# DLRM tower on one core: tables from the second on are split, loaded and awaited in one part instead of two, with the four orders laid out anew

## The reference, cut to what matters

```python
# 512 samples; 26 tables of 1000 to 125000 rows x 128, fp32
e = stack([tbl_f[ids[:, f]] for f in range(26)], axis=1)        # 512 x 26 x 128
combined = concatenate([dense[:, None, :], e], axis=1)          # 512 x 27 x 128
gram = einsum('bnd,bmd->bnm', combined, combined)               # 27 x 27 dot products per sample
z = concatenate([dense, gram[:, triu_i, triu_j], dense], axis=1)  # 128 + 351 + 128 = 607
h = maximum(z @ W_top1 + b_top1, 0)                             # 512 x 512
h = maximum(h @ W_top2 + b_top2, 0)                             # 512 x 256
y = h @ W_top3                                                  # 512 x 1
```

## Time and profile before

| what | value |
|---|---|
| median of 3 runs | 109.44 us (109.06 to 109.8) |
| profiled execution | 109.33 us |
| its span in the trace | 107.4 us |
| TensorE's granted clock | 1.0 of full speed throughout |

### The profile page before, as it was taken

How to read it: one execution, slowest core, us unless ns; L and a number is a source line. 1 busy time by engine, 2 the same in 40 slices (tenths; PEclk the granted TensorE clock), 3 DMA queues, 4 the chain that set the end, 5 groups by cost and what they waited for, 6 DMA issues and landing times.

```text
span 107.4 us, 3972 instructions
## 1 busy us (share of the span) xinstructions
PE 98.3 (92%) x1657; PEld 80.4 (75%) x1657; DVE 86.0 (80%) x255; ACT 64.4 (60%) x110; POOL 64.5 (60%) x68
## 2 busy tenths in 40 slices
PE   5969897997999899998999999999999997999991
PEld 2337576764766788877899887999798866998890
DVE  4799999999999999999999999999572436078121
ACT  5699989999999997809989474846300040001210
POOL 3577778777777778777777777777777700000000
PEclk9999999999999999999999999999999999999999
DMA  2999985747567847999782852112222110000000
GB/s 59 319 288 329 396 266 169 206 135 228 168 173 236 247 146 219 329 326 315 252 279 63 227 167 55 49 49 55 55 58 67 52 31 6 0 6 0 0 6 1
DMA packets 10575, 16.19 MB, mean 151 GB/s; under 512 B 2352, under 2 KB 6478, under 8 KB 10558
## 3 DMA queue, kind: packets, MB, share of 16 engines
q1 hardware_dynamic: 8398, 11.62, 34.0%
q0 software_dynamic: 2016, 4.13, 13.3%
q10 hardware_dynamic: 144, 0.19, 0.5%
HBM read 15.94 MB, written 0.00 MB: 148 GB/s over the span
## 4 chain that ended last, share of the span: by engine, by line
POOL 57%; issue 18%; PE 15%; DMA 6%; POOLq 1%; DVE 1%; DVEq 0%
POOL rows_sb L530 57%; PE h_ps L675 3%; DMA rows_sb<-in_tbl,ids_sb 3%; PE h_ps L650 3%; DMA ids_sb<-in_ids 2%; PE gram_ps L594 2%; PE h_ps L619 1%; PE turn_ps L650 1%; POOLq L293 1%; PE gram_ps L650 1%; PE turn_ps L619 1%; PE h_ps L658 1%; PE gram_ps L611 1%; PE turn_ps L594 1%; PE place_ps L611 0%
## 5 line engine op out<-in xcount | busy, mean ns | idle before, releaser
L530 POOL DMA_INDIRECT rows_sb<-in_tbl,ids_sb x63 | 63.6, 1009 | 20.9 <-issue 18.9
L571 PE MATMUL turn_ps<-onehot_sb,high_sb 128*128 128x512 f32 (+2 forms) x118 | 41.9, 367 | 3.5 <-DVE low_sb L807 1.4
L798 DVE TENSOR_SCALAR_CACHE_REDUCE onehot_sb<-lookup_ids_sb,first_sb 128x256 fp32r<-128x256 int16 (+2 forms) x79 | 43.6, 598 | 0.0
L572 PE MATMUL turn_ps<-onehot_sb,low_sb 128*128 128x512 f32 (+2 forms) x118 | 38.9, 342 | 0.0
L571 PEld LDWEIGHTS turn_ps<-onehot_sb,high_sb 128*128 128x128 f32 x118 | 22.2, 188 | 9.5 <-DVE low_sb L807 2.4
L572 PEld LDWEIGHTS turn_ps<-onehot_sb,low_sb 128*128 128x128 f32 x118 | 22.3, 189 | 1.6
L739 ACT ACTIVATE onehot_sb<-lookup_ids_sb,first_sb 128x512 fp32r<-128x512 int16 (+2 forms) x31 | 18.8, 621 | 2.3 <-PE turn_ps L572 2.2
L807 DVE TENSOR_TENSOR low_sb<-table_sb,high_sb 128x640 fp32r<-128x640 f32 (+1 forms) x26 | 19.4, 757 | 0.0
L729 ACT CAST high_sb<-table_sb 128x640 fp32r<-128x640 f32 (+1 forms) x26 | 17.0, 672 | 3.0 <-PE turn_ps L572 2.8
L594 PE MATMUL gram_ps<-feats 128*32 128x27 f32 x960 | 12.8, 196 | 1.1 <-DVE feats L701 0.4
L747 ACT ACTIVATE onehot_sb<-onehot_sb 128x768 fp32r<-128x768 f32 (+4 forms) x13 | 13.6, 1049 | 0.1
(11 more groups left out here) (53 smaller groups left out, 74.2 us busy)
## 6 DMA issues: line engine op xcount, KB each, us to landing
table_sb<-in_tbl SPq DMA_DIRECT2D x13, 256.0 KB, 3.5
table_sb<-in_tbl SPq DMA_DIRECT2D x7, 320.0 KB, 3.6
lookup_ids_sb<-in_lookup_ids SPq DMA_DIRECT2D x12, 128.0 KB, 2.4
table_sb<-in_tbl SPq DMA_DIRECT2D x6, 192.0 KB
rows_sb<-in_tbl,ids_sb POOLq DMA_INDIRECT x63, 3.3
w1p_sb<-in_w_pairs SPq DMA_DIRECT2D x1, 768.0 KB
w1d_sb<-in_w_dense SPq DMA_DIRECT2D x1, 512.0 KB, 6.3
w_sb<-in_w SPq DMA_DIRECT2D x1, 512.0 KB, 6.0
```

Source lines behind the costliest of these rows:

```text
L530: pool.indirect_dma_start(out=rows_sb[:, GATHERS.index((tile, slot)), :], out_offset=None, in_=tables[f], in_offset=bass.IndirectOffsetOnAxis(
L571: nc.tensor.matmul(bank, high_sb[0:rows, u % 2, c, :], picked, start=c == 0, stop=False)
L572: nc.tensor.matmul(bank, low_sb[0:rows, u % 2, c, :], picked, start=False, stop=c == CHUNKS[u] - 1).then_inc(chunk_used, 1)
L798: nc.vector.tensor_scalar(onehots(u, [c])[:, 0, :], lookup_ids_at(u), row_ids_sb[:, row:row + 1], None, ALU.is_equal, ALU.add, accum_out=m ...
```

## The change

`table_parts` gives one part for every table but the first. With it, for tables 1 to 12, the rows before the last chunk come with one DMA instead of two, both DMAs of a table count on one semaphore (one wait for 32), and there is one `cast`, one `low` and one wait of TensorE ahead of chunk 0. Table 0 keeps its two halves. The chunks that VectorE and ScalarE compare are the same in number. All four orders are written anew: among much else `turn 0 0` comes ahead of lookup 1, `turn 3 0` ahead of `lookup 12 8:10`, twins and `copy turn` steps elsewhere, `merge 3 0 16` ahead of `relu1 2`, `place 2` on VectorE ahead of `copy turn 3 4` and `layer3 1`, and on SP the loads of `dn`, `w1p`, `w1d`, `sm`, `w2` and `mask` between other tables. GpSimd's program is the same.

```diff
--- before.py
+++ after.py
@@ -113,18 +113,17 @@
 ONEHOT_MAX = max(n * (B - first * P) for n, first in zip(CHUNKS, LOOKUP_FROM))
 WARM_UPS = 12
 ACT_ROWS = 2 * NPAD
-ACT_CHUNKS = [2,3]*6+[3]
+ACT_CHUNKS = [2, 3] * 6 + [3]
 
 
 def table_parts(u):
 
-    return [range(0, CHUNKS[u] // 2), range(CHUNKS[u] // 2, CHUNKS[u])]
+    return [range(0, CHUNKS[u] // 2), range(CHUNKS[u] // 2, CHUNKS[u])] if u == 0 else [range(0, CHUNKS[u])]
 
 
 def dve_chunks(u):
 
-    first, second = table_parts(u)
-    return [first, range(second.start, CHUNKS[u] - ACT_CHUNKS[u])]
+    return [range(part.start, min(part.stop, CHUNKS[u] - ACT_CHUNKS[u])) for part in table_parts(u)]
 
 
 def act_chunks(u):
@@ -221,52 +220,49 @@
 
 
 PE_ORDER = """
-    lookup 0 0:8; lookup 1 0:8; turn 0 0; lookup 2 0:7; turn 0 1; lookup 2 7; lookup 3 0:3; turn 0 2; lookup 3
-    3:8; turn 0 3; lookup 4 0:8; turn 0 4; lookup 5 0:2; turn 1 0; lookup 5 2:8; lookup 6 0:4; gram 0 0 0;
-    lookup 6 4; gram 0 0 1; lookup 6 5:10; lookup 7 0; gram 0 1 0; lookup 7 1; turn 1 1; lookup 7 2:6; turn 1 2;
-    gram 0 1 1; lookup 7 6:10; lookup 8 0:4; place 0 0 32; lookup 8 4:6; turn 1 3; lookup 8 6:10; layer1 0 0 4;
-    turn 1 4; lookup 9 0:10; turn 2 0; lookup 10 0:2; gram 1 0 0; lookup 10 2; layer2 0 0; lookup 10 3:5; gram 1
-    0 1; lookup 10 5:10; gram 1 1 0; lookup 11 0:2; turn 2 1; lookup 11 2; gram 1 1 1; lookup 11 3:10; lookup 12
-    0:2; layer2 0 1; turn 2 2; turn 2 3; lookup 12 2:10; place 1 0 32; gram 2 0 0; gram 2 0 1; layer1 1 0 4;
-    gram 2 1 0; gram 2 1 1; layer2 1 0; turn 3 0; turn 3 1; turn 3 2; place 2 0 32; layer2 1 1; turn 3 3; turn 3
-    4; gram 3 0 0; gram 3 0 1; layer1 2 0 4; gram 3 1 0; gram 3 1 1; layer2 2 0; layer2 2 1; dense1 3 0 1;
-    dense1 3 1 2; place 3 0 16; place 3 16 32; bias2 3; dense1 3 2 3; dense1 3 3 4; layer1 3 0 1; layer1 3 1 2;
-    layer1 3 2 3; layer1 3 3 4; layer2 3 0; layer2 3 1
+    lookup 0 0:8; turn 0 0; lookup 1 0:8; lookup 2 0; turn 0 1; lookup 2 1:8; lookup 3 0:8; turn 0 2; lookup 4
+    0:4; turn 0 3; lookup 4 4:8; lookup 5 0:8; turn 0 4; lookup 6 0; gram 0 0 0; lookup 6 1:7; gram 0 0 1;
+    lookup 6 7:10; turn 1 0; lookup 7 0:4; gram 0 1 0; turn 1 1; lookup 7 4:6; gram 0 1 1; lookup 7 6:10; lookup
+    8 0:4; turn 1 2; lookup 8 4; turn 1 3; lookup 8 5; place 0 0 32; lookup 8 6:10; layer1 0 0 4; turn 1 4;
+    lookup 9 0:10; lookup 10 0:5; layer2 0 0; turn 2 0; gram 1 0 0; lookup 10 5; turn 2 1; lookup 10 6:8; gram 1
+    0 1; lookup 10 8:10; lookup 11 0; gram 1 1 0; lookup 11 1; layer2 0 1; lookup 11 2:4; turn 2 2; lookup 11
+    4:10; gram 1 1 1; lookup 12 0:4; turn 2 3; lookup 12 4:8; turn 3 0; lookup 12 8:10; place 1 0 32; gram 2 0
+    0; gram 2 0 1; layer1 1 0 4; gram 2 1 0; layer2 1 0; gram 2 1 1; turn 3 1; turn 3 2; layer2 1 1; place 2 0
+    32; turn 3 3; turn 3 4; gram 3 0 0; gram 3 0 1; layer1 2 0 4; gram 3 1 0; gram 3 1 1; dense1 3 0 1; layer2 2
+    0; layer2 2 1; place 3 0 16; dense1 3 1 2; place 3 16 32; dense1 3 2 3; bias2 3; dense1 3 3 4; layer1 3 0 1;
+    layer1 3 1 2; layer1 3 2 3; layer1 3 3 4; layer2 3 0; layer2 3 1
 """
 
 ACT_ORDER = """
-    distance 0 6; cast 0 0; distance 0 7; cast 0 1; distance 1 5; cast 1 0; distance 1 6; onehot 0; distance 1
-    7; onehot 1; cast 1 1; cast 2 0; distance 2 6; copy lookup 0; cast 2 1; distance 2 7; dense; cast 3 0;
-    onehot 2; cast 3 1; distance 3 5:7; copy turn 0 0; copy lookup 1; distance 3 7; copy turn 0 1; copy lookup
-    2; cast 4 0; onehot 3; distance 4 6:8; cast 4 1; cast 5 0; copy lookup 3; distance 5 5; cast 5 1; copy turn
-    0 3; distance 5 6; onehot 4; copy turn 0 2; distance 5 7; cast 6 0; copy lookup 4; distance 6 8; onehot 5;
-    copy turn 0 4; twin 0; distance 6 9; cast 6 1; cast 7 0; copy lookup 5; twin 1; distance 7 7; onehot 6; cast
-    7 1; distance 7 8:10; distance 8 8; cast 8 0; cast 8 1; onehot 7; copy lookup 6; copy lookup 7; distance 8
-    9; onehot 8; distance 9 7; cast 9 0; distance 9 8; copy turn 1 1; distance 9 9; place 0 0 32; onehot 9; copy
-    lookup 8; distance 10 8; copy turn 1 3; distance 10 9; onehot 10; cast 9 1; cast 10 0; cast 10 1; twin 2;
-    distance 11 7:9; cast 11 0; distance 11 9; cast 11 1; onehot 11; cast 12 0; copy lookup 9; cast 12 1; copy
-    lookup 10; distance 12 7; copy turn 2 1; distance 12 8; copy lookup 11; distance 12 9; onehot 12; twin 3;
-    copy turn 2 3; copy lookup 12; place 1 0 32; place 2 0 32; copy turn 3 1; copy turn 3 3; place 3 0 16; place
-    3 16 32; relu1 3 0 1; relu1 3 2 3
+    distance 0 6:8; cast 0 0; cast 0 1; onehot 0; distance 1 5:7; cast 1 0; distance 1 7; onehot 1; distance 2
+    6:8; cast 2 0; copy lookup 0; onehot 2; copy turn 0 0; distance 3 5:7; copy turn 0 1; cast 3 0; copy lookup
+    1; distance 3 7; dense; copy lookup 2; onehot 3; distance 4 6; cast 4 0; distance 4 7; onehot 4; cast 5 0;
+    copy lookup 3; copy turn 0 2; distance 5 5:8; onehot 5; copy lookup 4; distance 6 8; copy turn 0 3; cast 6
+    0; twin 0; distance 6 9; copy lookup 5; copy turn 0 4; cast 7 0; distance 7 7; onehot 6; distance 7 8:10;
+    cast 8 0; copy lookup 6; distance 8 8:10; copy turn 1 1; onehot 7; twin 1; twin 2; copy lookup 7; onehot 8;
+    cast 9 0; distance 9 7:9; place 0 0 32; twin 3; distance 9 9; copy lookup 8; distance 10 8; onehot 9;
+    distance 10 9; onehot 10; copy turn 1 3; cast 10 0; cast 11 0; copy lookup 9; distance 11 7:10; copy lookup
+    10; distance 12 7; copy turn 2 1; distance 12 8; cast 12 0; distance 12 9; onehot 11; copy lookup 11; onehot
+    12; copy turn 2 3; copy lookup 12; place 1 0 32; copy turn 3 1; copy turn 3 3; place 2 0 32; place 3 0 16;
+    place 3 16 32; relu1 3 0 1; relu1 3 2 3
 """
 
 DVE_ORDER = """
-    onehot 0 0:4; low 0 0; low 0 1; onehot 0 4; low 1 0; onehot 0 5; onehot 1 0:5; low 1 1; onehot 2 0:4; low 2
-    0; low 2 1; onehot 2 4:6; low 3 0; low 3 1; onehot 3 0:5; onehot 4 0; low 4 0; onehot 4 1:3; low 4 1; onehot
-    4 3:6; onehot 5 0:2; low 5 0; onehot 5 2:5; low 5 1; onehot 6 0:3; low 6 0; onehot 6 3:6; copy turn 1 0; low
-    6 1; onehot 6 6:8; onehot 7 0; low 7 0; onehot 7 1:4; low 7 1; onehot 7 4:7; onehot 8 0; merge 0 0 16;
-    onehot 8 1:4; low 8 0; onehot 8 4; merge 0 16 32; onehot 8 5; low 8 1; onehot 8 6:8; place 0 0 32; dense;
-    copy turn 1 2; onehot 9 0:4; low 9 0; onehot 9 4:7; low 9 1; low 10 0; onehot 10 0:2; copy turn 1 4; onehot
-    10 2:4; copy turn 2 0; relu1 0 0 4; low 10 1; onehot 10 4:8; onehot 11 0:2; low 11 0; onehot 11 2:6; low 11
-    1; onehot 11 6; low 12 0; onehot 12 0:6; low 12 1; onehot 12 6; merge 1 0 16; merge 1 16 32; copy turn 2 2;
-    place 1 0 32; merge 2 0 16; layer3 0; relu1 1 0 4; merge 2 16 32; copy turn 3 0; copy turn 3 2; copy turn 3
-    4; layer3 1; place 2 0 32; relu1 2 0 4; merge 3 0 16; merge 3 16 24; merge 3 24 32; layer3 2; place 3 16 32;
-    relu1 3 1 2; relu1 3 3 4; layer3 3
+    onehot 0 0:4; low 0 0; onehot 0 4; low 0 1; onehot 0 5; onehot 1 0:2; low 1 0; onehot 1 2:5; onehot 2 0:2;
+    low 2 0; onehot 2 2:6; onehot 3 0; low 3 0; onehot 3 1:5; onehot 4 0:2; low 4 0; onehot 4 2:6; onehot 5 0;
+    low 5 0; onehot 5 1:5; onehot 6 0:3; low 6 0; onehot 6 3:7; low 7 0; onehot 6 7; onehot 7 0:7; onehot 8 0:3;
+    low 8 0; onehot 8 3; copy turn 1 0; onehot 8 4; dense; onehot 8 5; merge 0 0 16; merge 0 16 32; onehot 8
+    6:8; onehot 9 0; place 0 0 32; copy turn 1 2; onehot 9 1:6; low 9 0; onehot 9 6; onehot 10 0:3; low 10 0;
+    onehot 10 3:5; relu1 0 0 4; onehot 10 5; copy turn 1 4; onehot 10 6:8; onehot 11 0:4; low 11 0; onehot 11 4;
+    copy turn 2 0; onehot 11 5:7; onehot 12 0:3; low 12 0; merge 1 0 16; onehot 12 3; copy turn 2 2; onehot 12
+    4:7; merge 1 16 32; place 1 0 32; layer3 0; copy turn 3 0; relu1 1 0 4; merge 2 0 16; merge 2 16 32; copy
+    turn 3 2; place 2 0 32; copy turn 3 4; layer3 1; merge 3 0 16; relu1 2 0 4; merge 3 16 24; merge 3 24 32;
+    layer3 2; place 3 16 32; relu1 3 1 2; relu1 3 3 4; layer3 3
 """
 
 SP_ORDER = """
-    ids; table 0; id; table 1; table 2; dn; w1d; table 3; table 4; table 5; table 6; mask; table 7; table 8;
-    table 9; w1p; table 10; sm; w2; table 11; table 12
+    ids; table 0; id; table 1; table 2; table 3; dn; table 4; table 5; w1p; table 6; w1d; table 7; table 8; sm;
+    w2; table 9; mask; table 10; table 11; table 12
 """
 
 
@@ -359,7 +355,8 @@
         dense_loaded = sem("dense_loaded")
         mask_loaded = sem("mask_loaded")
         lookup_ids_loaded = [sem(f"lookup_ids_loaded{u}") for u in range(LOOKUPS)]
-        table_loaded = [[sem(f"table_loaded{u}_{part}") for part in range(2)] for u in range(LOOKUPS)]
+        table_loaded = [[sem(f"table_loaded{u}_{part}") for part in range(len(table_parts(u)))]
+                        for u in range(LOOKUPS)]
         w1p_loaded = sem("w1p_loaded")
         w1d_loaded = sem("w1d_loaded")
         w2_loaded = sem("w2_loaded")
@@ -469,8 +466,8 @@
 
                 old = u - TABLE_BUFS
                 queue.wait_ge(onehot_act, done("act", "onehot", old))
```

(8 more changed lines are left out.)

## The result

The changed kernel takes 113.89 us (median of 4 runs, 112.9 to 116.03) against 109.39 us before: **slower by 3.8%**, ratio 1.0379 with a 95% interval of 1.0301 to 1.0458. The ratio leaves out the one execution of 116.03 us, which lies over 1.5% above the fastest of its kernel. The forecast was 112.3 us. Both profiled executions of the changed kernel (116.03 and, later, 116.07 us) are the longest of theirs and about 2 us above the median, so rows taken from them overstate what the median paid.

The account below looks back on a forecast made before the run. GpSimd's queue of gathers was taken as the bound, TensorE 0.25 us ahead. 109.33 + 3.2 (caught gathers) - 0.3 (tail) = 112.2 us, 112.3 by the median; forecast 110.8 to 114.0 (chance 0.70), whole range 109.7 to 114.3.

Parts of the forecast that it names:

- The bound: GpSimd's queue of 63 gathers ends last, TensorE's queue 0.25 us ahead; whatever lengthens the gathers' queue goes to the end in full.
- What holds a gather: A gather starting inside a remainder on VectorE (two SBUF inputs) waits for that instruction's end, then needs 0.82 us more.
- The caught time, +3.2 us: Delay of gathers starting inside remainders, on GpSimd's queue: 7.2 us after less 4.0 before, range 1.6 to 4.8.
- The saved 1.9 us of VectorE: Fixed part of 0.16 us per remainder, saved at most 12 times on VectorE; worth nothing ahead of the last gather.
- the first rival: Fewer VectorE operations make it faster: long remainders catch only 2.5 us, gathers land 1.5 us earlier, about 108.0 us; chance 0.09.
- the mean formula: Mean delay per remainder with random phase: w x w / (2 x 1.25) for caught stretch w below 1.25 us, else w - 0.62.
- Waits and buffers: Lookup's first chunk on TensorE waits for its whole table's cast and remainder, 2.9 us in all, hidden: cost 0.
- SP: SP's queue: one DMA issue fewer per table from the second on, loads moved, `ids` still first: cost 0.
- `turn 3 0`: On TensorE, moved ahead of `lookup 12 8:10`, waiting for the 52nd gather: cost 0, up to +0.5 us if a copy is late.
- The tail, -0.3 us: After the last gather, moving `merge 3 0 16` and `place 2` earlier on VectorE gives 0 to -0.6 us, -0.3 taken.
- A capped hold: Rival on GpSimd's gathers: caught ones wait at most 0.63 us, or fewer are caught; 109 to 110 us, chance 0.13.
- Starving: Rival: TensorE, waiting for whole tables, reaches `turn 3 4` behind the gathers; 114.3 us at 0.5 us per table, chance 0.08.

Follow-up runs that it names:

- before_merged: Kernel before, its orders, casts and loads kept, with only the two remainders of each of tables 1 to 12 merged into one: 120.9 us against 109.3.
- before_low2: Kernel before with each of its 26 remainders cut into two back-to-back pieces: 109.8 us, ratio 1.0067 to the kernel before.
- after_low4: Changed kernel with each merged remainder issued as four back-to-back pieces, all else merged: 111.36 us, ratio 1.0203 to the kernel before.
- after_parts2: Changed kernel's new orders with every table in two parts again (loads, casts, remainders, waits): 109.82 us, ratio 1.005 to the kernel before.
- before_tail: Kernel before with only the changed kernel's tail order on VectorE, TensorE's order as before: 108.98 us against 109.30, ratio 0.9964.

## Why the prediction was right, and where its numbers were not

- **The bound.** Right: the last gather was and is the end of the chain, and what was added to GpSimd's queue came out at the end.
- **What holds a gather.** Right and now shown: cutting the instruction takes the loss away (109.45), one input instead of two takes all catching away, and every caught gather of the changed kernel ends 0.81 to 0.83 us after its remainder, at 1.22 and 1.49 us as at 0.69.
- **The caught time, +3.2 us.** This term was mis-sized: 10.3 and 9.6 us were caught in the profiled executions instead of 7.2, so the queue grew by 6.3 and 5.6 us, above the range of 1.6 to 4.8 given for it. For the median an estimate is about 8.5 us caught, so +4.5: 113.9 less the 24.3 us from the last gather's start to the end, less 81.1 for an undisturbed queue from 3.5 us on. The step that failed is "I take the phase between the two queues as random". The next gather starts 1.12 us after the remainder ends (0.82 and 0.30), so each catch sets the phase anew, and VectorE's list decides the next: the remainders of tables 1 and 2 start 4.48 us apart, 4.48 - 1.22 - 1.12 = 2.14 = 1.25 + 0.89, and the gather after that one starts 0.36 us into the next remainder. The trace shows 0.37 us at 14.76 and again at 31.99, where the distance is the same 4.48. The same lengths in the old orders caught 5.7 us (`before_merged`), so what is caught depends on the order and not on the lengths alone. That the mean formula met the 4.0 us of the kernel before was in part luck: only 10 of its 26 remainders caught a gather for more than 0.02 us.
- **The saved 1.9 us of VectorE.** 1.5 us measured (19.4 to 17.9). "Worth nothing ahead of the last gather" holds in this direction. The other direction was left out of the prediction: TensorE, fed by VectorE, is only 0.25 us ahead, so what is added to VectorE's list soon counts (`before_low2` lost 0.7 us, `after_low4` 2.3). This also speaks against the first rival's 108.0 us: with no gather caught the new orders gave 109.7, though with VectorE 0.7 us busier than in the changed kernel; the merged remainders without any catch were not measured.
- **Waits and buffers, SP, `turn 3 0`: 0.** Right as a sum. TensorE's new waits, 6.6 us for gathers, are the late gathers themselves. VectorE now waits 3.3 us for casts, which the late gathers cover.
- **The tail, -0.3 us.** The moves on VectorE give it (0.3 us alone). The tail as a whole gained nothing (16.49 against 16.42 us), and the rows point to the dense rows laid singly on TensorE, which the prediction had not costed: 0 in the sum. So two terms were off, about +4.5 instead of +3.2 and 0 instead of -0.3; both made the forecast too low, by 1.6 us in all, and the time lies near the upper end of its 110.8 to 114.0.
- **Rivals.** A capped hold is refuted by the gather of 2.13 us. Starving is real in the old orders (120.9); in the new, TensorE's loader waits for a remainder once, 1.6 us.

## What to carry over

Before merging two VectorE instructions that read two tensors from SBUF, look whether GpSimd issues DMAs beside them on the path: what they cost there grows faster than their length, and an instruction cut in two may be cheaper than a whole one, until the engine's own list becomes the bound. Where two chains end within tenths of a microsecond of each other, cost each edit on both. And where one queue restarts at a fixed distance from the other's event, walk the phases along the order instead of averaging over them.

## What the runs showed beyond that

- One back-to-back pair of remainders lets a waiting gather through at the seam (1.30 us against 1.97 us for a gather that starts 0.34 us into a whole one).
- In the changed kernel TensorE's clock fell to the lower level (0.50) after waits of 1.68, 2.29 and 1.44 us for a gather, up to 18.46 us in the first profile and 30.68 and 93.87 in the second. It did not fall after one of 1.75 us up to 79.33 in the first: from 79.40 to 85.00 us it is 1.00. So the length of a single wait does not tell whether it falls. In a tail this cost 1.6 us.
- The last gather's landing varies: 2.4 to 2.5 us after its start in five of the ten traces, 3.1 to 3.6 in the others. In the kernel before it was 3.45, of which the last of the 16 completions took 0.96 us more than the one before it. Why is not shown.
- On one chip all four kernels stood still. VectorE's timeline of `before_tail` there, with the last gather issued at 82.52 us:

```profile
82.70 0.75 DVE L798 TENSOR_SCALAR_CACHE_REDUCE onehot_sb<-lookup_ids_sb,first_sb 128x512 fp32r<-128x512 int16 x1 [55.51 <-remote]
```

  The releaser is not named by the profile. It looks as if something did not land while the gathers were issued, but in `after_parts2` on the same chip a wait of VectorE of 41.16 us ended at 59.97 us, and gathers were issued there up to 81.58. What was waited for, and why on this chip alone, stays open.
